# The last attention's tail: turned tiles, one projection group and one norm group moved into the loop, two tiles per bank and another router order behind it

## What is computed

```python
h = h + _L1_attn_ref(_layernorm(h, axis=-1), L1_attn_Wqkv, L1_attn_Wproj, L1_attn_bproj)
h = h + _L1_ffn_ref(_layernorm(h, axis=-1), ...)

def _L1_attn_ref(x, Wqkv, Wproj, bproj):        # 12 heads of 16
    ...
    attn = jax.nn.softmax(jnp.einsum('bhqd,bhkd->bhqk', q, k) * SCALE, axis=-1)
    out = jnp.einsum('bhqk,bhkd->bhqd', attn, v)
    return out.transpose(0, 2, 1, 3).reshape(B, S, DIM) @ Wproj + bproj

def _L1_ffn_ref(x, W1, b1, W2, b2, Wr1, br1, Wr2, br2):
    h = jax.nn.relu(jnp.einsum('bsd,hd->bsh', x, Wr1) + br1)      # router, hidden
    score = jnp.einsum('bsd,ed->bse', h, Wr2) + br2               # router, gate
    _, idx = jax.lax.top_k(score, K)
    ...
```

## Time and profile before

| what | us |
|---|---|
| median of 3 runs | 1839.52 (1836.33 to 1840.29) |
| the profiled execution | 1839.05 |
| its span | 1837.2 |
| last attention loop's end, tail's first turn | 1524.13 |
| last gate product done | 1591.57 |
| PE busy over the span | 1475.5 (80%) |
| DVE, ACT, POOL busy | 1241.6, 978.1, 809.0 |

### The profile page before, as it was taken

One profiled execution on the slowest core, in us unless ns is written; L12 is line 12 of the kernel. 1 busy time (PEld: TensorE's weight loads), 2 busy tenths in 40 slices (PEclk: granted clock), 3 DMA queues, 4 the chain that ended last, 5 costly groups with the idle time before them and its releaser, 6 DMA issues.

```text
span 1837.2 us, 42512 instructions
## 1 busy us (share of the span) xinstructions
PE 1475.5 (80%) x13098; PEld 1248.7 (68%) x13098; DVE 1241.6 (68%) x3530; ACT 978.1 (53%) x2392; POOL 809.0 (44%) x1177
## 2 busy tenths in 40 slices
PE   0588889789798888989888948849949987679994
PEld 0377678677676776777776827719937765569994
DVE  4698966879775989668896662253368997434444
ACT  0478733688434886338883213225528993135552
POOL 5577323675235773247742320024537521135551
PEclk9899989999899998999998967768969996679997
DMA  3265201734005460026430000036625420157774
GB/s 89 66 148 123 42 1 30 177 80 95 1 1 138 87 144 12 1 47 158 97 76 1 1 14 1 1 147 181 192 85 127 90 62 26 56 178 240 242 247 136
DMA packets 121981, 167.27 MB, mean 91 GB/s; under 512 B 21776, under 2 KB 81232, under 8 KB 121616
## 3 DMA queue, kind: packets, MB, share of 16 engines
q1 hardware_dynamic: 114448, 147.19, 31.6%
q0 software_dynamic: 7296, 17.18, 2.8%
HBM read 128.27 MB, written 36.04 MB: 89 GB/s over the span
## 4 chain that ended last, share of the span: by engine, by line
PE 31%; DVE 12%; issue 5%; ACT 2%; DMA 2%; POOL 2%; SPq 0%; POOLq 0%; DVEq 0%; ACTq 0%
PE bank L1462 7%; DVE neg_max L789 3%; PE bank L1448 2%; PE bank L643 2%; PE bank L1449 1%; PE bank L1452 1%; PE bank L1451 1%; PE bank L1450 1%; DVE xn L909 1%; DVE ptl L796 1%; PE bank L1214 1%; PE bank L561 1%; PE bank L429 1%; PE bank L1435 1%; DVE xx L763 1%
## 5 line engine op out<-in xcount | busy, mean ns | idle before, releaser
L683 ACT ACTIVATE prob<-bank,neg_max 128x192 f32<-128x192 f32 (+1 forms) x960 | 362.0, 433 | 75.9 <-DVE neg_max L789 64.2
L789 DVE TENSOR_REDUCE neg_max<-bank 128x2 f32<-128x384 f32 (+1 forms) x480 | 274.6, 573 | 45.6 <-PE bank L542 42.2
L796 DVE TENSOR_TENSOR ptl<-bank,pth 128x384 f16<-128x384 f32 (+1 forms) x480 | 274.2, 571 | 39.1 <-ACT pth L696 25.0
L561 PE MATMUL bank<-ident,prob 128*128 128x128 f32 x1536 | 270.3, 290 | 0.0
L696 ACT ACTIVATE pth<-bank 128x384 f16<-128x384 f32 (+1 forms) x480 | 249.6, 520 | 35.0 <-PE bank L561 30.2
L650 ACT ACTIVATE xx<-bank 128x256 fp32r<-128x256 f32 x256 | 94.5, 383 | 191.1 <-PE bank L429 187.2
L542 PE MATMUL bank<-kx,qx 96*128 96x192 bf16 (+1 forms) x960 | 167.9, 257 | 1.1 <-DVE xx L763 1.1
L561 PEld LDWEIGHTS bank<-ident,prob 128*128 128x128 f32 x1536 | 164.1, 144 | 0.1
L582 PE MATMUL bank<-v,pth 128*128 128x33 bf16 x1152 | 138.6, 180 | 16.9 <-DVE ptl L796 12.0
L540 PE MATMUL bank<-mask,ident 128*128 128x384 bf16 x384 | 130.5, 340 | 20.7 <-DMA kx<-qk_rows 11.8
L731 ACT ACTIVATE fbuf<-bank,b 128x512 f32<-128x512 f32 x96 | 65.6, 687 | 146.1 <-PE bank L451 146.1
(11 more groups left out here) (293 smaller groups left out, 4515.6 us busy)
## 6 DMA issues: line engine op xcount, KB each, us to landing
xn<-in_e_seg SPq DMA_DIRECT2D x34, 768.0 KB, 6.5
w<-in_e_w SPq DMA_DIRECT2D x23, 576.0 KB, 4.2
qk_rows<-fbuf SPq DMA_DIRECT2D x128, 96.0 KB, 2.3
qx<-qk_rows SPq DMA_DIRECT2D x35, 288.0 KB, 4.0
kx<-qk_rows SPq DMA_DIRECT2D x35, 288.0 KB, 5.8
qk_rows<-w SPq DMA_DIRECT2D x80, 96.0 KB, 2.3
qx<-qk_rows SPq DMA_DIRECT2D x35, 192.0 KB, 4.7
kx<-qk_rows SPq DMA_DIRECT2D x35, 192.0 KB, 5.6
```

What stands on the lines that cost most here:

```text
L561: last = nc.tensor.transpose(bank[BT[p % 2]][:, c * P:c * P + P], probs_at(p, banded, c * P, P), ident[:, :])
L683: nc.scalar.activation(probs_at(p, banded, qt * n, n), scores_at(p, n)[:, qt, :], ACT.Exp, bias=neg_max[:, b % 2, hd, qt:qt + 1], scale=1. ...
L789: nc.vector.tensor_reduce(neg_max[:, b % 2, hd, :], scores_at(p, D if banded else S), AX.X, ALU.max, negate=True).then_inc(max_ready.sem, 1)
L796: nc.vector.tensor_tensor(ptl[:, p % 2, 0:n], bank[BT[p % 2]][:, 0:n], pth[:, p % 3, 0:n], ALU.subtract)\
```

## The change

`LATE` holds for the last attention as well (the test on `banded` is gone from `step`). Its tiles 0 to 7 are turned at pairs 70 to 76 and 86 to 92, tiles 0 to 3 are projected at 78 to 84, group 0 gets its statistics at pair 88 and its norm, one of eight pieces a pair, at pairs 94 to 101. `late` gives the place in the semaphores' count. POOL makes group 0's scale before its last three attention scalings.

Behind the loop a table `LAST` gives the order for PE and ACT; DVE has a list of its own. Two tiles are turned into one bank by four transposes (`pe_turn_two`), copied by one ACT operation of 512 columns and split by two DVE operations of 256 (`act_split_two`, `dve_split_two`); a turn waits until the pair of tiles before last is split. The gate of a group no longer stands behind the next group's hidden layer in all cases: gate 0 follows hidden 1, gate 1 hidden 2, gate 2 stands behind the turn of norm 3, hidden 3 and gate 3 come last.

```diff
+LAST = (("att", 2), ("out", 1), ("norm", 0), ("att", 3), ("out", 2), ("hidden", 0), ("out", 3), ("norm", 1), ("hidden", 1),
+        ("gate", 0), ("norm", 2), ("hidden", 2), ("gate", 1), ("norm", 3), ("gate", 2), ("hidden", 3), ("gate", 3))
...
+        def late(it, banded, t):
+
+            return (it, turned(1, t)) if banded else (L + 1, last_turn(0, t))
+
+        def two_at(s):
+
+            return bank[BX[s // 2 % 2]][:, :].rearrange("p (t a n) -> p t a n", t=2, a=2)
+
         def step(p, banded):
...
-            if banded and p in LATE:
+            if p in LATE:
...
+        def pe_turn_two(pe, it, s, t, src, ready, turn, n):
+
+            pe.wait_ge(ready.sem, ready.at(turn, n))
+            pe.wait_ge(xx_ready.sem, xx_ready.at(it, s - 2))
+            for i in range(2):
+                for c in range(2):
+                    last = nc.tensor.transpose(two_at(s)[:, i, c, :], src[:, t + i, c * P:c * P + P], ident[:, :])
+            last.then_inc(xt_done.sem, 2)
...
+        def act_split_two(act, it, s, t):
+
+            act.wait_ge(xt_done.sem, xt_done.at(it, s + 2))
+            nc.scalar.activation(xx[:, 0:2, t * P:t * P + 2 * P].rearrange("p a (t n) -> p t a n", t=2), two_at(s),
+                                 ACT.Copy).then_inc(xh_ready.sem, 2)
...
+        def dve_split_two(dve, it, s, t):
+
+            dve.wait_ge(xh_ready.sem, xh_ready.at(it, s + 2))
+            ps, tk = two_at(s), slice(t * P, t * P + 2 * P)
+            part = lambda a: xx[:, a, tk].rearrange("p (t n) -> p t n", t=2)
+            nc.vector.tensor_tensor(part(2), ps[:, :, 0, :], part(0).bitcast(F32), ALU.subtract)
+            nc.vector.scalar_tensor_tensor(part(1), in0=part(1).bitcast(F32), scalar=lo_rows[:, :], in1=ps[:, :, 1, :],
+                                           op0=ALU.mult, op1=ALU.add).then_inc(xx_ready.sem, 2)
...
-            if banded and p == LATE[2 * GT - 1] + 4:
+            if p == LATE[2 * GT - 1] + 4:
                 dve_stats(dve, ch, it, 0, 0, o_read)
             if banded:
                 dve_norm_step(dve, ch, it, p - LATE[2 * GT - 1] - 10, NORMED.index((1, 0)) + 1, 0, 0)
+            elif 0 <= p - LATE[2 * GT - 1] - 10 < 2 * GT:
+                dve_normalise(dve, ch, L + 1, NG + 1, 0, [p - LATE[2 * GT - 1] - 10])
...
             for f in range(NT - 5, NT):
+                if f == NT - 3:
+                    pool_rstd(pool, ch, L + 1, NG + 1, 0, 1e-5)
                 pool_scale(pool, L, f)
-            for g in range(NG):
+            for g in range(1, NG):
                 pool_rstd(pool, ch, L + 1, NG + g + 1, g, 1e-5)
...
+            dve_last("att", 2)
+            dve_last("out", 1)
+            dve_last("norm", 0)
+            dve_last("att", 3)
+            dve_normalise(dve, ch, L + 1, NG + 2, 1)
+            dve_last("out", 2)
+            dve_last("out", 3)
+            dve_last("norm", 1)
+            dve_normalise(dve, ch, L + 1, NG + 3, 2)
+            dve_last("norm", 2)
+            dve_normalise(dve, ch, L + 1, NG + 4, 3)
+            dve_last("norm", 3)
```

More of the change, by code:

```diff
@@ L404, in pe_step @@
                 elif kind == "att":
-                    pe.wait_ge(xx_ready.sem, xx_ready.at(it, turned(1, a) + 1))
+                    n, s = late(it, banded, a)
+                    pe.wait_ge(xx_ready.sem, xx_ready.at(n, s + 1))
                 else:
@@ L719, in act_attention @@
                     elif kind == "att":
-                        act_split(act, it, turned(1, a), a, True)
+                        act_split(act, *late(it, banded, a), a, True)
         def act_hidden(act, it, b1, sigs, func, before):
@@ L747, in dve_step @@
                 elif kind == "att":
-                    dve_split(dve, it, turned(1, a), a, True)
+                    dve_split(dve, *late(it, banded, a), a, True)
                 elif kind == "out":
-                    dve.wait_ge(hb_ready.sem, hb_ready.at(it, normed(2, a) - 2 * NT))
+                    dve.wait_ge(hb_ready.sem, hb_ready.at(it, normed(2, a) - 2 * NT if banded else a + 1))
                     dve.wait_ge(o_done.sem, o_done.at(it, a + 1))
@@ L1877, in _ @@
             act_attention(act, L, False, xn_split)
-            for g in range(NG + 3):
-                if g < NG:
-                    for t in range(GT * g, GT * g + GT):
-                        act_split(act, L + 1, last_turn(0, t), t)
-                if 2 <= g < NG + 2:
-                    for t in range(GT * (g - 2), GT * (g - 1)):
-                        act_split(act, L + 1, last_turn(1, t), t)
-                if g >= 3:
+            for kind, g in LAST:
+                tiles = range(GT * g, GT * g + GT)
+                if kind == "att":
+                    for t in tiles[::2]:
+                        act_split_two(act, L + 1, last_turn(0, t), t)
+                elif kind == "norm":
+                    for t in tiles[::2]:
+                        act_split_two(act, L + 1, last_turn(1, t), t)
+                elif kind == "hidden":
                     for s in range(2):
-                        act.wait_ge(r_done.sem, r_done.at(0, 2 * (g - 3) + s + 1))
-                        act.wait_ge(g2_done.sem, g2_done.at(0, GT * (g - 4)))
+                        act.wait_ge(r_done.sem, r_done.at(0, 2 * g + s + 1))
+                        act.wait_ge(g2_done.sem, g2_done.at(0, GT * (g - 1)))
                         m = P if s == 0 else D2
-                        nc.scalar.activation(fbuf[0:m, 2 * ((g - 3) % 2) + s, :], bank[BR[s]][0:m, :], ACT.Relu,
+                        nc.scalar.activation(fbuf[0:m, 2 * (g % 2) + s, :], bank[BR[s]][0:m, :], ACT.Relu,
                                              bias=br1[0:m, s:s + 1]).then_inc(r_ready.sem, 1)
@@ L2106, in _ @@
                 pe_open(pe, L, kind, i, wb, xn_turn, lambda n: (L, 2 * NT + n))
[L2107 to L2119 removed]
+            pe_attention(pe, L, False, wb, xn_turn, lambda n: (L, 2 * NT + n), wa)
@@ new lines, in _ @@
+            for kind, g in LAST:
+                tiles = range(GT * g, GT * g + GT)
+                if kind == "att":
+                    for t in tiles[::2]:
+                        pe_turn_two(pe, L + 1, last_turn(0, t), t, xn, att_ready, L, t + 2)
+                elif kind == "out":
+                    pe_out(pe, L, wa, 0, g, lambda t: (L + 1, last_turn(0, t) + 1))
+                elif kind == "norm":
+                    for t in tiles[::2]:
+                        pe_turn_two(pe, L + 1, last_turn(1, t), t, xn, xn_ready, 0, 3 * NT + t + 2)
+                elif kind == "hidden":
+                    if g == 0:
@@ L2120, in _ @@
                         pe.wait_ge(seg_q_ready.sem, seg_q_ready.at(0, 3))
[L2121 removed]
+                    pe.wait_ge(xx_ready.sem, xx_ready.at(L + 1, last_turn(1, GT * g + GT - 1) + 1))
                     for s in range(2):
[L2123 to L2124 removed]
@@ L2125, in _ @@
-                if g >= 4:
-                    pe.wait_ge(r_ready.sem, r_ready.at(0, 2 * (g - 3)))
-                    for t in range(GT * (g - 4), GT * (g - 3)):
+                        pe.wait_ge(r_ready.sem, r_ready.at(0, 2 * (g - 1) + s + 1))
+                        pe_features(bank[BR[s]][:, :], wb, s * P, g).then_inc(r_done.sem, 1)
+                else:
+                    pe.wait_ge(r_ready.sem, r_ready.at(0, 2 * (g + 1)))
+                    for t in tiles:
                         tk = slice(t % GT * P, t % GT * P + P)
-                        f = 2 * ((g - 4) % 2)
+                        f = 2 * (g % 2)
```

62 lines of the change are left out of this document (24 added, 38 removed).

## The result

| | median, us | range, us | runs |
|---|---|---|---|
| before | 1837.91 | 1834.49 to 1841.28 | 17 |
| changed | 1827.06 | 1822.33 to 1837.63 | 17 |

The ratio is 0.9950, with a 95% interval from 0.9936 to 0.9963, so the change is worth 6.8 to 11.8 us. The forecast was 7.7. The profiled execution of the changed kernel took 1827.66 us, with a span of 1825.8 against 1837.2: 11.4 less.

The account below looks back on a forecast made before the run. ACT and DVE were taken to bound the loop's end, PE the tail behind it. Tail 45.2 work plus 9.0 waits is 54.2, gaining 13.2 us; less 5.5 for the loop gives 7.7, so 1831.4 us, range 1826.0 to 1836.5.

Parts of the forecast that it names:

- The loop: Last attention loop's end: added turned tiles, projections, statistics and normalising pieces cost 5.5 us, bounds 3.9 and 8.
- PE's five waits: Tail behind the loop: PE's waits in the new order, hand-scheduled, sum to 9.0 us.
- Fourth tile of projection 2: Tail: PE waits 1.4 us for a residual that DVE has queued behind normalising group 1.
- Hidden 1: Tail: PE waits 2.6 us for norm 1, behind DVE's statistics of group 3.
- Hidden 2: Tail: PE waits 2.0 us for norm 2's chain of copy, split and handover.
- Gate 3: Tail's end: gate 3 directly follows hidden 3, so PE waits 1.1 us for Relu and handover.
- The joined turns: Tail: a joined ACT copy takes 0.62 us, a joined DVE split of two tiles 0.8 us.
- PE's work: Tail: 45.2 us, 56% of the way from 31.6 at the high clock to 56 at the low (low price).
- A: Loop absorbs more (3.9 us), fewer waits give PE the high clock more often (tail 51); 1826.5 us; chance 0.16.
- B: Joined handovers keep the time (tail 56.5), loop steps cost 0.6 each (loop 8); 1836.1 us; chance 0.19.
- C: Clock stays low throughout the tail, gate products standing between dense groups; tail 64 us, 1841.2 us; chance 0.07.
- D: Path not shortened, since the last products behind the tail hang on something else; chance under 0.01.

Follow-up runs that it names:

- e10: The changed kernel run once more, unedited, on one chip with e9, e11 and e12; 1828.67 us, ratio to before 0.9956.
- e9: Changed kernel with two pairs swapped in PE's order: gate 0 ahead of hidden 1, gate 1 ahead of hidden 2; 1819.79 us, ratio to before 0.9911.
- e1: Kernel before plus only the change's steps in the loop; behind it the old order and single-tile turns; 1831.35 us, ratio to before 0.9969.
- e5: Changed kernel with 46 unread identity transposes put into PE's five waits behind the loop; 1825.65 us, ratio to before 0.9926.
- e6: e4 with 22 unread identity transposes ahead of group 3's first turn and projection 2's fourth tile; 1816.38 us, ratio to before 0.9878.
- e11: The kernel of e4 run once more, on one chip with e9, e10 and e12; 1819.04 us, ratio to before 0.9909.
- e3: Changed kernel with one tile in a bank again behind the loop, new order kept; 1837.61 us, ratio to before 0.9990.
- e4: Changed kernel with the old order behind the loop, joined turns and the loop's steps kept; 1815.19 us, ratio to before 0.9885.
- e7: Changed kernel with a third order behind the loop, other PE work between each turn and the product reading it; 1819.38 us, ratio to before 0.9905.
- e12: The kernel of e7 run once more, on one chip with e9, e10 and e11; 1816.59 us, ratio to before 0.9893.
- e8: e4 without the loop's steps: groups 0 and 1 turned, group 0 projected and normalised behind the loop; 1826.07 us, ratio to before 0.9927.

## Why the prediction was right, step by step

**The loop: 5.5 us forecast, 5.7 measured** (45.54 less 40.11 to pair 95, and 0.24 in the drain), and 0.7 less in e10. The terms inside were less good. Three turned tiles cost 9.37 less 8.37 = 1.00, 0.33 each, as in the banded loop and not the 0.48 that I took from one tile; a single one cost 0.52 again. Three projected tiles cost 0.27 where I had put nothing. The six pairs with a projected tile, two turned ones and the statistics cost 2.10; less two turned tiles at 0.33 and 0.09 for the projection that leaves 1.35 for the statistics, where I took 1.13. The last five pairs cost 8.17 less 6.63 = 1.54, and 7.48 less 6.63 = 0.85 in e10. Two turned tiles are 0.66 of that, so the first normalising pieces some 0.2 (forecast 0.3), and 0.7 in the first execution is the clock (last section). Too much for turned tiles, 3.8 against 2.8, too little for projections, statistics and clock, and the errors met.

**PE's five waits: 9.0 us forecast, 8.96 and 8.06 measured.** Behind the first turn of group 3: 1.9 forecast, 1.81 measured. Fourth tile of projection 2: 1.4 and 2.35. Hidden 1: 2.6 and 2.44. Hidden 2: 2.0 and 1.59. Gate 3: 1.1 and 0.77. The second was missed because I priced PE's turns and three products at 4.5 us. They took 3.0, with the clock high; DVE's chain didn't get shorter, so the wait grew. e10 shows it from the other side: there the same work took 4.5, its products at the low level, and the wait was 0.86, and work and wait together are 5.4 us in both. For such sums: a high clock ahead of a wait that DVE ends is paid back in it.

**The joined turns.** The copy took 0.60 (0.62 forecast). A joined split took 0.42 and 0.47, from start to start 0.73 (from 1538.95 to 1539.68 in the timeline of DVE), where I had 0.8.

**PE's work: 45.2 us forecast, 41.4 and 46.0 measured** (tail less waits less the 0.3 at each of them). This was the term with the real uncertainty, and one trace of before didn't show it: 40% and 59% of the way to the low price where I had 56%. The tail, forecast 54.2, was 51.9 and 55.85 in two executions. That 54.2 lies between them is in part luck, for nothing in the sum says which mixture an execution meets.

**The sum.** 7.7 us forecast; 10.85 between the medians, 8.1 between those of e10's chip. The predicted 1831.4 is 4.3 above the median, and the bounds held it.

**The rivals.** The median stands next to A's 1826.5, but not by A's way: the loop took 5.7 and not 3.9, and the clock behind the loop was low until 1534 in the execution shown, the dense run of turns, projection 1 and norm 0 notwithstanding. What A says of the clock (fewer waits, more often high) holds between the orders with joined turns: from e10 to e9, 8.06 less 4.93 = 3.1 us of waits went and 9.1 of PE's busy time, from the first execution of the changed kernel to e9 4.0 and 4.2. It does not hold everywhere: e1 has 3.4 us of waits less than before and the same clock, 0.68. The Trainium skill (TensorE: Matmul & The Clock Gate, What's actually happening) has activity release the throttled state; e5's added work (clock 0.86 after 0.76 and 0.66) agrees, e6's (0.86 as in e11) shows nothing of it, and in e9 the clock fell though PE had been busy throughout. B fails: the joined handovers cost nothing more (split directly behind the copy), and steps in the loop under 0.55 each. C's price for a low clock (64 us) was nearly met by e3, 62.2 at 0.64, whose median is 10.5 us above the changed kernel's and level with before. Its reason, the gate products between the dense groups, is where the clock fell in most cases (see e9); the changed kernel's two executions, at 0.76 and 0.66, stayed on the better side of its price. D is excluded by DVE's 9.93 us of idleness, ended by the last gate product.

**What it missed.** The forecast took the change as one thing and asked whether it gains. It never priced the new order by itself against the old one with joined turns. The five waits were all in my sum, 9.0 us. The same hand schedule on the old order should have shown the two ahead of hidden products and the one ahead of gate 3 gone; e4 measured 4.9 us in all.

## What to carry to other kernels

Between turning a tile and the product that reads it put other work of PE, longer than the split's way over the two other engines. Even tiny products take the wait away, but in e9 the clock fell behind them. A wait of PE can go with more lost time than its length: the nine executions with the same unfilled work in the tail (changed, e1, e3, e4, e7, e9 to e12) run from 41.4 us with 3.3 of waits to 62.2 with 10.8, some 3 us of tail for each us of wait. That is a trend over different programs and not a price: of one program, the execution with 0.9 us of waits less had the tail that was 4 us longer. Take a change of several parts apart; the joined turns and the loop's steps were hiding a new order that cost 9 to 12 us.

## What the hardware showed that was not expected

The same program meets the clock differently in each execution, while most of its waits stay. From pair 12 to pair 66 all fourteen executions took 81.62 to 81.74 us, and PE's busy time in the tail of one program was 42.84 and 47.70. In kernels whose code up to pair 70 is one and the same, pair 12 starts anywhere from 1391.6 (e9) to 1400.8 (e8). That difference of 9 us arises ahead of the last attention's loop; from what, no run here tells, and in a single trace it can hide or feign a gain as large as this change's.

The steps in the loop also lower the clock inside it. In the kernel before the granted clock is 1.00 up to pair 95; in the changed one there is a low stretch behind the statistics:

```profile
1515.00:1521.00 6.00, 6.00 (x69) 5.44 (x70) 5.30 (x13) 4.63 (x12) 0.88 (x2) 0.50 0.01 3
```

It is there in each kernel with the loop's part and in none without. It lasted some 7 us in the first execution of the changed kernel, in e1 and in e4, whose loops took 45.5 us, and some 3 in the other eight, whose loops took 44.7 to 45.1. DVE is the full engine there, and still 3.5 us more at the low level cost about 0.6.

The clock also falls where PE doesn't stand still: behind gate products, with no wait for 8 us ahead (e9), and with all five waits shortened or filled (e5, from 1559.3, behind gate 0). Filling the waits with 46 transposes that nobody reads went with 5 to 10 us less busy time for the same real work in e5, and filling two of them with 22 in e6 with none.
